# Attention scores of the 64-wide heads: fp32 products over 64 rows in the two row halves of the array, instead of split products over 128 rows

## The reference

```python
q = _lora_proj(x, Wq, qA, qB).reshape(b, s, NQ, HD).transpose(0, 2, 1, 3)   # NQ 16, HD 64
k = _lora_proj(x, Wk, kA, kB).reshape(b, s, NKV, HD).transpose(0, 2, 1, 3)  # NKV 4
...
q = _rope(q, cos_h, sin_h)
k = _rope(k, cos_h, sin_h)
...
attn = jax.nn.softmax(jnp.einsum('bhqd,bhkd->bhqk', q, k) * ATTN_SCALE, axis=-1)
out = jnp.einsum('bhqk,bhkd->bhqd', attn, v)
```

## Time and profile before

| | us |
|---|---|
| median of the runs | 2506.13 |
| lowest run | 2504.76 |
| span of the profiled execution, first to last instruction | 2505.2 |
| first S of this stage | 40.38 |
| first S of the last step | 852.75 |
| PE busy in 100 to 200 us | 99.54 of 100 |

### The profile page before, as it was taken

One profiled execution on the slowest core, in us unless ns is written; L12 is line 12 of the kernel. 1 busy time (PEld: TensorE's weight loads), 2 busy tenths in 40 slices (PEclk: granted clock), 3 DMA queues, 4 the chain that ended last, 5 costly groups with the idle time before them and its releaser, 6 DMA issues. The chain is left out here.

```text
span 2505.2 us, 37039 instructions
## 1 busy us (share of the span) xinstructions
PE 2115.1 (84%) x13722; PEld 1255.3 (50%) x13732; DVE 1604.2 (64%) x3493; ACT 1412.2 (56%) x2024; POOL 780.1 (31%) x426
## 2 busy tenths in 40 slices
PE   4999999999999935758727786999979747999798
PEld 3666666666666522612323544444446623444467
DVE  5887787887877556631256655877623686777324
ACT  3777776777777543269752343466653252566541
POOL 3887776877867401142101203100000022000000
PEclk8999999999999966879957897799989875999899
DMA  2000000000000050062050211311010003210100
GB/s 75 1 5 1 3 5 1 1 3 5 1 3 1 1 172 0 8 164 58 1 172 1 69 49 46 83 40 40 2 34 1 1 21 80 48 40 21 35 1 18
DMA packets 44484, 82.10 MB, mean 33 GB/s; under 512 B 9106, under 2 KB 18026, under 8 KB 41658
## 3 DMA queue, kind: packets, MB, share of 16 engines
q1 hardware_dynamic: 44306, 79.74, 11.5%
HBM read 64.09 MB, written 14.88 MB: 32 GB/s over the span
## 5 line engine op out<-in xcount | busy, mean ns | idle before, releaser
L807 ACT ACTIVATE probs<-psum_banks 128x1024 f32<-128x1024 f32 (+1 forms) x416 | 381.2, 979 | 247.5 <-PE psum_banks L675 146.8
L1238 POOL TENSOR_SCALAR l0a_rows<-l0a_rows,l0a_rinv 128x1024 f32<-128x1024 f32 x160 | 454.3, 2844 | 188.4 <-DVE l0a_rinv L1200 184.7
L886 DVE TENSOR_REDUCE neg_max<-psum_banks 128x1 f32<-128x512 f32 (+3 forms) x672 | 406.7, 659 | 154.0 <-PE psum_banks L709 90.4
L1188 DVE TENSOR_REDUCE l0a_nmax<-psum_banks 128x1 f32<-128x1024 f32 x256 | 312.4, 1220 | 137.4 <-PE psum_banks L1082 135.6
L671 PE MATMUL psum_banks<-q_stack,k_stack 75*128 75x512 bf16 (+7 forms) x1216 | 279.4, 341 | 52.2 <-ACT probs L807 23.7
L1134 ACT ACTIVATE l0a_rows<-psum_banks,l0a_nmax 128x1024 f32<-128x1024 f32 x256 | 285.8, 1116 | 60.9 <-DVE l0a_nmax L1188 59.5
L705 PE MATMUL psum_banks<-k_stack,q_stack 72*128 72x128 bf16 (+3 forms) x1024 | 249.5, 330 | 38.9 <-DMA q_stack<-q_parts 35.8
L1096 PE MATMUL psum_banks<-packed,l0a_rows 128*128 128x128 f32 x2048 | 267.2, 273 | 2.7 <-POOL l0a_rows L1238 1.6
L1096 PEld LDWEIGHTS psum_banks<-packed,l0a_rows 128*128 128x128 f32 x2048 | 239.2, 141 | 42.9 <-issue 5.4
L1081 PE MATMUL psum_banks<-l0a_kh,l0a_qw 128*128 128x512 f32 x512 | 241.7, 472 | 19.2 <-POOL l0a_qw L1227 13.3
L691 PE MATMUL psum_banks<-probs,v_ones 128*32 128x512 f32 (+3 forms) x2432 | 239.9, 506 | 9.5 <-ACT o_sum L778 6.5
(11 more groups left out here) (289 smaller groups left out, 3521.5 us busy)
## 6 DMA issues: line engine op xcount, KB each, us to landing
q_stack<-q_parts SPq DMA_DIRECT2D x21, 576.0 KB
k_stack<-k_parts SPq DMA_DIRECT2D x42, 192.0 KB
qkv<-in_l0f_w SPq DMA_DIRECT2D x6, 1024.0 KB, 5.5
moe_b<-in_l0f_b SPq DMA_DIRECT2D x32, 128.0 KB, 3.6
k_stack<-k_eight SPq DMA_DIRECT2D x16, 256.0 KB
l1f_w<-in_l1f_w SPq DMA_DIRECT2D x16, 256.0 KB, 4.7
q_stack<-q_parts SPq DMA_DIRECT2D x32, 96.0 KB
q_parts<-parts SPq DMA_DIRECT2D x12, 256.0 KB
```

Of the source, the lines that this page charges most:

```text
L807: act.activation(S.Pt[:, U % PBUFS, 2 * half:2 * half + 2, c0:HALF], PS[:, bank:bank + 2, c0:HALF], ACT.Exp).then_inc(exp_done, 1)
L886: dve.tensor_reduce(out, scores, AX, ALU.max, negate=True).then_inc(job_read, 1)
L1188: dve.tensor_reduce(R.nmax4[:, s % 4:s % 4 + 1], scores(s), AX, ALU.max, negate=True).then_inc(max_done, 1)
L1238: rows_divided.mark(pool.tensor_scalar(R.Pr[:, s % RING, :], R.Pr[:, s % RING, :], R.rinv4[:, s % 4:s % 4 + 1], None, ALU.mult))
```

## The change

Queries and keys stay whole fp32 numbers. POOL writes its sum straight to its place: `R.K` has the keys in both 64-row halves as before, `R.Q` has a pair of heads one above the other. A second tile, `R.Qx`, has the pair with its halves exchanged; two transfers on SP's queue fill it, 64 rows x 512 each, for each of the 32 query units. A step has two fp32 matmuls over 64 rows. The first 512 keys use rows 0 to 63 of the array and the last 512 keys rows 64 to 127, each into its own bank. A head reads its own half from `R.Q` and the other half from `R.Qx`. The steps `high` on ACT and `low` on POOL are gone, and PE waits for the sum and for the transfers.

```diff
-    def targets(u):
...
+    def place(u):
...
+            return R.K[:, w % B, n]
+        return R.Q[:, REP // 2 * (w % B) + k // 2 - 1, n]
...
         @block.sync
         def _(sp):
...
+            for u, n in query_no.items():
+                w, k = units[u]
+                sp.wait_ge(summed, u + 1)
+                if n >= 2:
+                    sp.wait_ge(*swap_landed(n - 2))
+                for own, other in (halves, halves[::-1]):
+                    sp.dma_start(swap_of(u)[other], place(u)[own]).then_inc(swapped[n % 2], 16)
+                g = (w + 1) // B
+                if k == 4 and w % B == 1 and g < NKV:
...
+                    sp.dma_start(R.W[:], D["l0a_w"][g]).then_inc(w_loaded, 16)
...
+                elif k == 5 and w % B == 0 and w:
+                    sp.wait_ge(job_ready, number["out", w - 1, 1] + 1)
...
                     if s % NT == 0:
                         u = unit_no[s // STEPS, 2 + s % STEPS // NT]
-                        pe.wait_ge(hi_done, u + 1)
-                        pe.wait_ge(lo_done, low_parts(u))
+                        pe.wait_ge(summed, u + 1)
+                        pe.wait_ge(*swap_landed(query_no[u]))
                     if s >= 2:
                         pe.wait_ge(exp_done, s - 1)
-                    for c0 in (0, HALF):
-                        pe.matmul(scores(s)[:, c0:c0 + HALF], q, R.Kh[:, b, c0:c0 + HALF], start=True, stop=False)
-                        m = pe.matmul(scores(s)[:, c0:c0 + HALF], q, R.Kl[:, b, c0:c0 + HALF], start=False, stop=True)
+                    for i, rows in enumerate(halves):
+                        q = (R.Q if i == own else R.Qx)[rows, pair, j * P:(j + 1) * P]
+                        to = slice(i * HALF, (i + 1) * HALF)
+                        m = pe.matmul(scores(s)[:, to], q, R.K[rows, b, to], start=True, stop=True)
                     m.then_inc(rows_ready, 1)
...
         @block.scalar
         def _(act):
-            def high(u):
-                act.wait_ge(summed, u + 1)
-                for rows, hi, lo in targets(u):
-                    ins = act.activation(hi, R.t_cos[rows, u % 3, :], ACT.Copy)
-                ins.then_inc(hi_done, 1)
...
         @block.gpsimd
         def _(pool):
...
                 for u in sums_at.get(s, ()):
-                    total_of(u)
-                    if s < 0:
-                        low(u)
-                for u in lows_at.get(s, ()) if s >= 0 else ():
-                    low(u)
+                    pool.wait_ge(job_read, number["rope", *units[u]] + 1)
+                    pool.tensor_tensor(place(u), R.t_cos[:, u % 3, :], R.t_sin[:, u % 3, :], ALU.add).then_inc(summed, 1)
```

More of the change, by code:

```diff
@@ L971, in wide_heads @@
     done_at = [step_of["rope", *u] for u in units]
-    sums_at, highs_at, lows_at = {}, {}, {}
+    sums_at = {}
     for n, s in enumerate(done_at):
         sums_at.setdefault(s + 3 if s >= 0 else s, []).append(n)
-        highs_at.setdefault(s + 5 if s >= 0 else s, []).append(n)
-        lows_at.setdefault(s + 5 if s >= 0 else s, []).append(n)
+    query_no = {u: n for n, u in enumerate(u for u in range(len(units)) if units[u][1] >= 2)}
+    halves = slice(0, HD), slice(HD, P)
     def item(s):
@@ L994, in bank_of, with swap_of, swap_landed @@
         return 4 + n % 4 if n < lead else SPARE
-    def targets(u):
+    def place(u):
         w, k = units[u]
-        b, n = w % B, slice(k % 2 * HALF, (k % 2 + 1) * HALF)
+        n = slice(k % 2 * HALF, (k % 2 + 1) * HALF)
         if k < 2:
[L1002 to L1008, removed]
+            return R.K[:, w % B, n]
+        return R.Q[:, REP // 2 * (w % B) + k // 2 - 1, n]
+    def swap_of(u):
+        w, k = units[u]
+        return R.Qx[:, REP // 2 * (w % B) + k // 2 - 1, k % 2 * HALF:(k % 2 + 1) * HALF]
+    def swap_landed(n):
+        return swapped[n % 2], 32 * (n // 2 + 1)
     def scale_of(job):
@@ L1018, in wide_heads @@
     with phase(S, 18) as (block, (rows_ready, max_done, exp_done, inv_done, pool_normed, act_normed, turned, act_copied,
-                                  dve_copied, pv_done, o_read, job_ready, job_read, summed, hi_done, lo_done,
+                                  dve_copied, pv_done, o_read, job_ready, job_read, summed, even_swapped, odd_swapped,
                                   w_loaded, o_loaded)):
+        swapped = even_swapped, odd_swapped
         def scores(s):
@@ L1025, in _ @@
         def _(sp):
[L1026 to L1033, removed]
+            for u, n in query_no.items():
+                w, k = units[u]
+                sp.wait_ge(summed, u + 1)
[5 more added lines that the diff above has]
+                if k == 4 and w % B == 1 and g < NKV:
+                    last = max(number[job] for job in order if job[0] in ("rope", "value") and job[1] == w)
+                    sp.wait_ge(job_ready, last + 1)
+                    sp.dma_start(R.W[:], D["l0a_w"][g]).then_inc(w_loaded, 16)
+                    sp.dma_start(R.lb[:], D["l0a_lb"][g]).then_inc(w_loaded, 16)
+                elif k == 5 and w % B == 0 and w:
+                    sp.wait_ge(job_ready, number["out", w - 1, 1] + 1)
+                    sp.dma_start(R.wo[:], D["l0a_wo"][g]).then_inc(o_loaded, 16)
+                    sp.dma_start(R.oa[:], D["l0a_oa"][g]).then_inc(o_loaded, 16)
         @block.tensor
@@ L1072, in _ @@
                     hh, j = item(s)
-                    q, b = R.Qw[:, hh, j * P:(j + 1) * P], s // STEPS % B
+                    pair, own, b = hh // 2, hh % 2, s // STEPS % B
                     if s % NT == 0:
                         u = unit_no[s // STEPS, 2 + s % STEPS // NT]
-                        pe.wait_ge(hi_done, u + 1)
-                        pe.wait_ge(lo_done, low_parts(u))
+                        pe.wait_ge(summed, u + 1)
+                        pe.wait_ge(*swap_landed(query_no[u]))
                     if s >= 2:
                         pe.wait_ge(exp_done, s - 1)
-                    for c0 in (0, HALF):
-                        pe.matmul(scores(s)[:, c0:c0 + HALF], q, R.Kh[:, b, c0:c0 + HALF], start=True, stop=False)
-                        m = pe.matmul(scores(s)[:, c0:c0 + HALF], q, R.Kl[:, b, c0:c0 + HALF], start=False, stop=True)
+                    for i, rows in enumerate(halves):
+                        q = (R.Q if i == own else R.Qx)[rows, pair, j * P:(j + 1) * P]
+                        to = slice(i * HALF, (i + 1) * HALF)
+                        m = pe.matmul(scores(s)[:, to], q, R.K[rows, b, to], start=True, stop=True)
                     m.then_inc(rows_ready, 1)
@@ L1144, in _ @@
                                    scale=R.rinv4[:, r % 4:r % 4 + 1]).then_inc(act_normed, 1)
-                for u in highs_at.get(s, ()):
-                    high(u)
         @block.vector
@@ L1170, in read @@
                     if u >= 3:
-                        dve.wait_ge(hi_done, u - 2)
-                        dve.wait_ge(lo_done, low_parts(u - 3))
+                        dve.wait_ge(summed, u - 2)
                     dve.scalar_tensor_tensor(R.t_cos[:, u % 3, :], PS[:, bank, :], scale_of(job),
@@ L1213, in _ @@
         def _(pool):
[L1214 to L1227, removed]
+            rows_divided = Chain(pool, pool_normed)
             for s in range(-1, total):
                 for u in sums_at.get(s, ()):
-                    total_of(u)
-                    if s < 0:
-                        low(u)
-                for u in lows_at.get(s, ()) if s >= 0 else ():
-                    low(u)
+                    pool.wait_ge(job_read, number["rope", *units[u]] + 1)
+                    pool.tensor_tensor(place(u), R.t_cos[:, u % 3, :], R.t_sin[:, u % 3, :], ALU.add).then_inc(summed, 1)
                 if s >= 0 and not on_act(s):
@@ L1246, in __init__ @@
         self.V = S.sb("l0a_v", [P, B, NT, HD])
-        self.Kh, self.Kl = S.sb("l0a_kh", [P, B, T], F32R), S.sb("l0a_kl", [P, B, T], F32R)
-        self.Qw = S.sb("l0a_qw", [P, B * REP, T], F32R)
+        self.K = S.sb("l0a_k", [P, B, T])
+        self.Q, self.Qx = (S.sb(f"l0a_{x}", [P, B * REP // 2, T]) for x in ("q", "qx"))
         self.nmax4, self.rsum4, self.rinv4 = (S.sb(f"l0a_{x}", [P, 4]) for x in ("nmax", "rsum", "rinv"))
```

## The result

The changed kernel takes **2543.5 us** (median of four runs, 2541.9 to 2544.3); the kernel before took 2505.5 beside it (median of four; one of them, 2920.6, is left out of the ratio). The ratio is 1.0149, with a 95% interval from 1.0127 to 1.0171: slower by 1.5%, less than the 2% that was called a measurable change. 2549 was forecast, within 2522 to 2578. The profiled execution has a span of 2540.2 us, 35.0 more than before.

The account below looks back on a forecast made before the run. PE was taken to bound the steady state, so its added work counts one to one: 2505.2 + 46.2 (array) - 2 (start of the stage) = 2549.4, forecast 2549 us, range 2522 to 2578.

Parts of the forecast that it names:

- S, 0.07 us saved: Score matmuls of a step: two fp32 pairs side by side take 0.86 us instead of 0.93.
- The staircase: Rival: array takes score instructions strictly in order, three places instead of two, +105.8, 2655 us; chance 0.13.
- the case without overlap: Rival: the score matmuls' row halves do not overlap at all, four places, 2761 us; chance 0.02.
- S to T, 0.16: From 64-row scores to 128-row turnings: 0.10 us gap plus 0.06 for first weights, 246 times, +39.4 us.
- Into S, 0.20: From turnings into 64-row scores: 0.20 us for gap and uncovered weights, 120 times, +24.0 us.
- No price for the shape: Rival: changing matmul shape between scores and turnings costs nothing, 2486 us, not slower; chance 0.05.
- The rest of the edits, nothing in the steady state: Work taken from ACT and POOL gains nothing in the steady state, since PE does not wait for them.
- The start, -2: Start of the stage: first S -0.6 and step 8 -1.2, together -2 us, within -3 to +4.
- near 897: Sign that the forecast is right: the last step's S starts near 897 us.
- the array's own part: PE's matmuls in the steady state: +39.4, +24.0 and -17.2, together +46.2 us.

Follow-up runs that it names:

- experiment 2: Changed kernel with both matmuls of a step on rows 0 to 63, so nothing can lie side by side; 2769.7 us.
- experiment 1: Changed kernel with the score matmuls over all 128 rows, the sum of two heads' scores being computed; 2686.5 us.
- experiments 4: Changed kernel with keys, queries and copied queries as fp32r, one pass for each matmul, at less precision; 2416.2 us.
- experiments 5: Changed kernel with T (the turnings) in 64-row halves too, each half into its own bank, so S and T share one shape; 2467.7 us.
- 7: Changed kernel with two steps' S (score matmuls) together: S, S, T, PV, T; 2584.0 us.
- Experiment 8: The kernel before, with ACT's copy of a finished output placed ahead of the step's other work; 2498.6 us.
- 9: Changed kernel with ACT's copy of a finished output placed ahead of the step's other work; 2543.1 us.
- experiment 3: Changed kernel without the two transfers a unit and the wait for them, so the other head's scores are computed; 2539.2 us.

## Why the prediction was right, step by step

- *S, 0.07 us saved.* Right: two places side by side, 0.86 for 0.93. The staircase and the case without overlap fell with the first rows; experiment 2 shows what no overlap would have cost. The Trainium skill's rule, "TensorE: Matmul & The Clock Gate", Part 3, What overlaps and what doesn't, that matmuls start and end strictly in program order, holds here for the two matmuls of a step taken whole: the first half's starts first (380.72 against 380.73). It does not hold for their instructions if these stand as the kernel gives its matmuls, both of the first half ahead of both of the second: then the second half's first instruction passes the first half's second, which starts 0.53 later. The profile does not show the order in the queue itself.
- *S to T, 0.16.* The right mechanism, a little too dear: 0.147 (a gap of 0.09, where I had read 0.10 from bf16 rows, and 0.056 for T's first weights; medians over the stage). 246 x 0.013 = 3.2 us.
- *Into S, 0.20.* 0.198, a gap of 0.094 and 0.104 for the first weights. The forecast read it from S after PV, and that row held.
- *No price for the shape.* Experiments 1, 2, 4 and 5 and the rows of 7 speak against it. "TensorEngine Tiling (Array Packing)", Key Properties, in the Trainium skill says that a change of tiling mode drains TensorE; the traces agree (the gap of 0.09 us), and add that the next weights are not loaded ahead either, which is about as large a part as the gap.
- *The rest of the edits, nothing in the steady state.* This is the step that failed, and it is the largest single part of what I was off. I had the 6.0 us of waits in the earlier trace rows and called them small, but in the changed kernel they are nearly gone, and I did not subtract them. Experiment 8 shows that they are worth 6 to 7 us in the kernel before, and 9 that 1.3 are left in the changed one: 5.4 in the stage. Which of the two removed them, the longer step or the ACT freed of its roundings, was not tried by itself. But experiments 4 and 5 have ACT freed too, with shorter steps, and there the 13 waits are back, 7.3 and 5.4 us: a freed ACT alone does not remove them, which speaks for the longer step.
- *The start, -2.* -1.5 at step 10 in this pair of profiles. That it comes so near is chance: 1.2 of it lay ahead of the change's own work, and in the pair of experiments 8 and 9 step 10 comes 2.0 later in the changed kernel (67.66 and 69.62). What the start is worth is not told within 2 us either way. The two transfers landed together, as taken: S starts 3.11 after the sum, where the row of the same size gave 3.6. The later ones are hidden, as said (experiment 3).

Together: of the forecast's +44.2 the array's own part is 4.5 less (41.7 for 46.2), the waits take 5.4, and the start gives 0.5 less than forecast. That is +34.8; the span grew by 35.0. The last S came at 887.6 and not near 897, for the same reasons.

## What to carry to other kernels

Count how often neighbouring matmuls change their shape in rows, and price each change (here 0.15 to 0.2 us) before splitting a matmul into row tiles: a split that saves 0.07 us a step can lose twice that and more at its borders. If the split is wanted, give the neighbours the same shape, and then look what the new order makes wait. Small waits of the bounding engine belong into the sum too: work added to that engine can swallow them.

## What the runs showed of the hardware that was not expected

- Sixteen turnings of 64 x 64, in the two row halves, take 0.49 us from first start to the next matmul of the same shape; eight of 128 x 128 take 0.87 (experiments 5 and 1).
- With one 64-row half of the array in use (experiment 2) the granted clock stood at 0.50, the 1.2 GHz level, from 40 to 90 us while PE had no idle time:

```profile
40.00:60.00 20.00, 20.00 (x24) 7.23 (x23) 8.39 (x11) 5.86 (x9) 5.69 (x2) 0.50 0.00 0
60.00:80.00 20.00, 20.00 (x47) 10.73 (x46) 7.69 (x13) 5.85 (x9) 6.92 (x3) 0.50 0.06 13
80.00:100.00 20.00, 20.00 (x38) 8.71 (x36) 10.19 (x15) 7.86 (x12) 8.91 (x4) 0.54 0.06 14
100.00:120.00 20.00, 20.00 (x85) 8.99 (x84) 14.17 (x22) 10.70 (x17) 8.94 (x5) 1.00 0.06 14
```

With whole 128 rows (experiment 1) it was 0.94 and 1.00 in the first two of these stretches. Later, with T and PV between, both ran at 1.00. But both row halves do not keep it up by themselves: the changed kernel also stood at 0.50 from 53 to 65 us, with PE busy for all of these 12 us. Which condition held the clock down, the one half or something else of this stretch, was not tried.

At that clock a place takes 0.86, so two more of them in each of the first ten steps are 17 us. That experiment 2 lost just these 17 us between its first S and step 10 (46.7 us against 29.8) is partly chance: it has no idle time there, where the changed kernel waits for 5.3 us, and its other work ran slower by about as much.
